# Division of attention's sums moved to GpSimd, with its other work and the steps of three chains placed anew

## What is computed

```python
xn = (x - mean(x)) / sqrt(var(x) + 1e-5)
q = rope((xn @ Wqa @ Wqb).reshape(b, s, 16, 8))
k, v = split((xn @ Wkva @ Wkvb).reshape(b, s, 4, 8, 2))   # 4 heads of k and v serve 16 of q
w = softmax(where(causal, -inf, q @ k.T * 8 ** -0.5))
attn = (w @ v).reshape(b, s, 128) @ Wout + bout
# fp4 quantization in blocks of 16 of the last dimension, of activations and weights
scale = max(max|block| / 6, 1e-12); q4 = GRID[searchsorted(MID, |block / scale|)] * sign * scale
h = silu(q4(xn) @ q4(w_gate).T) * (q4(xn) @ q4(w_up).T)    # 352 wide
out = x + attn + q4(h) @ q4(w_down).T
```

## Time and profile before

| | us |
|---|---|
| median of 3 runs | 797.62 |
| lowest and highest | 795.21, 798.21 |
| the profiled execution's own time | 797.94 |
| its span, first to last instruction | 795.9 |

### The profile page before, as it was taken

How to read it: one execution, slowest core, us unless ns; L and a number is a source line. 1 busy time by engine, 2 the same in 40 slices (tenths; PEclk the granted TensorE clock), 3 DMA queues, 4 the chain that set the end, 5 groups by cost and what they waited for, 6 DMA issues and landing times.

```text
span 795.9 us, 18365 instructions
## 1 busy us (share of the span) xinstructions
PE 722.8 (91%) x6453; PEld 442.3 (56%) x6453; DVE 644.0 (81%) x1390; ACT 535.1 (67%) x1154; POOL 612.3 (77%) x708
## 2 busy tenths in 40 slices
PE   2467889999999999999999999999999999998986
PEld 1233455665656565665656565565656665665434
DVE  6569788989888888989888988889888988878412
ACT  2213686867777777777776767777776867676672
POOL 5534597878889797878889797878889797856662
PEclk9998899999999999999999999999999999999998
DMA  4423233233334343243334343343434333341111
GB/s 113 115 68 88 73 86 102 86 108 110 96 92 116 104 118 96 89 117 98 103 99 119 88 116 96 91 115 96 108 99 116 87 117 93 93 102 38 56 49 35
DMA packets 85028, 75.48 MB, mean 95 GB/s; under 512 B 28642, under 2 KB 67010, under 8 KB 84938
## 3 DMA queue, kind: packets, MB, share of 16 engines
q1 hardware_dynamic: 84938, 74.32, 34.3%
HBM read 40.45 MB, written 27.25 MB: 85 GB/s over the span
## 4 chain that ended last, share of the span: by engine, by line
PE 39%; POOL 32%; ACT 11%; DVE 7%; issue 6%; DMA 3%; SPq 2%; POOLq 0%; DVEq 0%; ACTq 0%
PE pv_ps L1160 10%; POOL P L554 9%; PE exp_ps L1139 7%; POOL h L564 5%; PE max_ps L1124 5%; ACT P L961 5%; POOL h L567 5%; POOL h L570 4%; PE misc_ps L1184 3%; PE max_ps L1125 3%; PE misc_ps L1192 3%; DVE neg_max L737 3%; PE misc_ps L1209 3%; POOL q_split L645 2%; POOL rstd L596 2%
## 5 line engine op out<-in xcount | busy, mean ns | idle before, releaser
L737 DVE TENSOR_REDUCE neg_max<-max_ps 128x1 f32<-128x512 f32 (+3 forms) x768 | 429.9, 593 | 87.1 <-PE max_ps L1125 85.2
L961 ACT ACTIVATE P<-exp_ps 128x512 f32<-128x512 f32 x512 | 294.9, 599 | 167.7 <-PE exp_ps L1139 166.6
L1139 PE MATMUL exp_ps<-Q,K 128*128 128x512 bf16 (+3 forms) x1024 | 244.0, 301 | 10.3 <-ACT P L961 6.5
L1124 PE MATMUL max_ps<-K,Q 128*128 128x384 bf16 (+2 forms) x768 | 199.2, 278 | 18.9 <-DMA Kd<-K 11.7
L1125 PE MATMUL max_ps<-Kd,Q 128*128 128x128 bf16 x1024 | 191.3, 221 | 2.1 <-DVE neg_max L737 2.0
L554 POOL TENSOR_SCALAR_AFFINE_SELECT P<-P 128x512 f32<-128x512 f32 x256 | 161.8, 667 | 26.8 <-ACT P L964 26.8
L1160 PE MATMUL pv_ps<-P,V 128*32 128x512 f32 (+3 forms) x2048 | 163.9, 438 | 1.9 <-POOL P L554 0.8
L1124 PEld LDWEIGHTS max_ps<-K,Q 128*128 128x128 bf16 x768 | 75.9, 100 | 93.3 <-DVE neg_max L737 47.2
L1125 PEld LDWEIGHTS max_ps<-Kd,Q 128*128 128x128 bf16 x1024 | 98.4, 100 | 46.1 <-issue 22.7
L1139 PEld LDWEIGHTS exp_ps<-Q,K 128*128 128x128 bf16 x1024 | 79.7, 98 | 48.4 <-ACT P L961 27.1
L585 POOL TENSOR_TENSOR h<-gate_sb,up_half 128x352 f32<-128x352 f32 x64 | 59.6, 932 | 58.7 <-DVE gate_sb L750 58.6
(11 more groups left out here) (128 smaller groups left out, 974.1 us busy)
## 6 DMA issues: line engine op xcount, KB each, us to landing
Q<-q_scr SPq DMA_DIRECT2D x64, 224.0 KB
o_scr<-oT SPq DMA_DIRECT2D x31, 256.0 KB, 2.6
q_scr<-q_split SPq DMA_DIRECT2D x16, 384.0 KB, 2.6
Kd<-K SPq DMA_DIRECT2D x64, 96.0 KB
x_in<-x SPq DMA_DIRECT2D x16, 256.0 KB, 4.5
q_scr<-q_split SPq DMA_DIRECT2D x16, 256.0 KB, 2.9
x_res<-x SPq DMA_DIRECT2D x16, 256.0 KB, 5.7
out<-y SPq DMA_DIRECT2D x32, 128.0 KB, 4.3
```

The costliest lines, as they stand in the source:

```text
L737: nc.vector.tensor_reduce(neg_max[:, pr // 4, heads[0]:heads[0] + len(heads), pr % 4, i], max_ps[r % 3][:, 0:len(heads) * n].rearrange("p ...
L961: nc.scalar.activation(P[g % 2][:, hh + r % 2, col:col + 512], ps[:, :], ACT.Exp, scale=SCALE).then_inc(exp_done, 1)
L1124: nc.tensor.matmul(ps[:, col:col + d], Qt, Kt[:, half, g, 0:d], start=True, stop=True)
L1139: last = nc.tensor.matmul(exp_ps[n % 2][:, col:col + width], K[par][:, half, pr // 2, kb * 128:(kb + 1) * 128], Q[par][:, pr, kb * 128:S], ...
```

## The change

- GpSimd no longer makes var_eps, neg_mean, shift, the copies of V and x_bias; of the statistics it keeps the power. VectorE makes var_eps (slot 3) and shift (slot 4's end, one instruction).
- The division `onT` goes from VectorE (slot 5) to GpSimd, ahead of the fourth h product.
- GpSimd's step 0 on h stands ahead of the first h product, not behind x's steps 1 to 3.
- V has three buffers, and VectorE copies v from PSUM straight into it, in two instructions; v_stage goes.
- bout becomes row 96 of the third chunk of the down projection's weights, with a row of ones in hqT, set once on VectorE. x_res is added directly, and SP loads it in the pass that uses it.
- ScalarE's powers of h go from behind tiles (2, 2), (2, 3), (2, 4), (3, 2) to (1, 0), (1, 2), (1, 4), (2, 2), x's from (0, 0) to (0, 2). The pieces of xn go from tiles 0 to 3 to tiles 0, 2, 3, 4 of slot 5.
- On VectorE the second half of h's magnitudes stands behind the maxima of tiles 3 and 4 of slot 4, two of four bn_stats at the end of slot 1, and hidden_max(T, 2) in slot 5.

The diff, without the declarations of tiles and semaphores:

```diff
@@ -64,7 +64,7 @@
-H_POWERS = [(2, 2), (2, 3), (2, 4), (3, 2)]
+H_POWERS = [(1, 0), (1, 2), (1, 4), (2, 2)]
 PV_BLOCKS = ((0, 3), (1, 2))
@@ -347,7 +346,7 @@
             for dst, src in (
-                (bout_sb[:, :], bout.partition_broadcast(128)),
+                (wdT[FC[2][1]:FC[2][1] + 1, 2, :], bout.unsqueeze(0)),
                 (w_raw[:, 768:768 + F], wdown),
@@ -475,11 +474,13 @@
+                    T.prev().misc_wait(sp, misc_read, "out1")
+                    sp.dma_start(x_res[:, :, :], x[T.batch(-1)].rearrange("(c p) e -> p c e", p=128)).then_inc(x_res_loaded, 16)
                     return finish()
-                if T.has(0):
...
-                    T.wait(sp, x_bias_done, 1, 0, 0)
-                    sp.dma_start(x_res[:, :, :], x[T.batch(0)].rearrange("(c p) e -> p c e", p=128)).then_inc(x_res_loaded, 16)
+                if T.has(-1):
...
+                    T.prev().misc_wait(sp, misc_read, "out1")
+                    sp.dma_start(x_res[:, :, :], x[T.batch(-1)].rearrange("(c p) e -> p c e", p=128)).then_inc(x_res_loaded, 16)
                 scatter_sums(T, -1, 1)
@@ -585,17 +586,23 @@
-            def statistics(T):
+            def normalize(T):
...
+                if not T.has(-1) or T.t0 == LAST_T:
+                    return
+                T.wait(pool, o_loaded, 32, -1, 32)
+                T.wait(pool, o_inv_in, 32, -1, 32)
+                if T.has(-2):
...
+                    T.prev().misc_wait(pool, misc_filled, "out1")
+                nc.gpsimd.tensor_tensor(onT[:, :], o_raw[:, :], o_spread[:, :], ALU.mult).then_inc(o_normed, 1)
...
+            def deviation(T):
...
                     return
-                T.wait(pool, mv_done, NT, 3, NT)
-                nc.gpsimd.tensor_scalar(var_eps[:, :], bn_mv[:, :, 1], EPS, None, ALU.add).then_inc(var_done, 1)
-                nc.gpsimd.tensor_scalar(neg_mean[:, :], bn_mv[:, :, 0], -1.0, None, ALU.mult).then_inc(var_done, 1)
-                T.wait(pool, var_done, 2, 3, 2)
+                T.wait(pool, var_done, 1, 3, 1)
                 nc.gpsimd.tensor_tensor(rstd[:, :], var_eps[:, :], half_neg[:, :], ALU.pow).then_inc(rstd_done, 1)
-                T.wait(pool, rstd_done, 2, 3, 1)
-                nc.gpsimd.tensor_tensor(shift[:, :], neg_mean[:, :], rstd[:, :], ALU.mult).then_inc(rstd_done, 1)
@@ -605,6 +612,8 @@
                 split_rest(T, 0, 1)
+                if T.has(0):
+                    quantize(T, 0, 0, *hs)
                 hidden(T, 0)
@@ -613,21 +622,11 @@
                     nc.gpsimd.tensor_tensor(blocks(w_raw[:, :]), blocks(w_raw[:, :]), spread(w_inv[:, :]), ALU.mult).then_inc(w_step, 1)
-                if T.has(0):
-                    quantize(T, 0, 0, *hs)
                 hidden(T, 1)
...
                     causal(T, 0, 0)
-                if T.has(1):
...
-                    T.prev().misc_wait(pool, misc_read, "v")
-                    if T.has(-1):
-                        T.wait(pool, pv_done, KVH, -1, KVH)
-                    for s in range(2):
-                        nc.gpsimd.tensor_copy(V[T.par(1)][:, :, s::2, D * s:D * s + D],
-                                              v_stage[:, :, :].rearrange("p c (g d) -> p c g d", g=KVH)[:, :, s::2, :]).then_inc(v_ready, 1)
                 if T.has(2):
@@ -650,8 +649,9 @@
                     nc.gpsimd.tensor_tensor(k_split[:, 2, :], k_rest[:, :], k_split[:, 1, :], ALU.subtract).then_inc(k_pool, 1)
-                statistics(T)
+                deviation(T)
                 split_rest(T, 1, 0)
+                normalize(T)
                 hidden(T, 3)
@@ -661,11 +661,6 @@
                     quantize(T, 0, 3, *hs)
-                if T.has(0):
-                    T.wait(pool, x_res_loaded, 16, 0, 16)
-                    T.misc_wait(pool, misc_read, "out1")
-                    nc.gpsimd.tensor_tensor(x_bias[:, :, :], x_res[:, :, :],
-                                            bout_sb[:, :].unsqueeze(1).to_broadcast([128, NT, E]), ALU.add).then_inc(x_bias_done, 1)
                 if T.has(3):
@@ -689,14 +684,20 @@
-            def magnitudes(eng_wait, mag, sem_):
...
+            def magnitude_bits(mag, sem_):
                 m = mag.bitcast(U16)
...
                 nc.vector.tensor_scalar(m, m, 0x7F80, 0x0040, ALU.bitwise_and, ALU.bitwise_or).then_inc(sem_, 1)
...
+            def magnitude_floor(eng_wait, mag, sem_):
...
                 eng_wait(sem_, 1)
                 nc.vector.tensor_scalar(mag, mag, 1.5 * 2.0 ** 22, None, ALU.max).then_inc(sem_, 1)
...
+            def magnitudes(eng_wait, mag, sem_):
...
+                magnitude_bits(mag, sem_)
+                magnitude_floor(eng_wait, mag, sem_)
@@ -767,28 +768,17 @@
-            def normalize(T):
...
-                if not T.has(-1):
-                    return
-                T.wait(dve, o_loaded, 32, -1, 32)
-                T.wait(dve, o_inv_in, 32, -1, 32)
-                if T.has(-2):
...
-                    T.prev().misc_wait(dve, misc_filled, "out1")
-                nc.vector.tensor_tensor(onT[:, :], o_raw[:, :], o_spread[:, :], ALU.mult).then_inc(o_normed, 1)
...
             def output(T, n):
...
                 if n == 0:
-                    T.wait(dve, x_bias_done, 1, -1, 1)
+                    T.wait(dve, x_res_loaded, 16, -1, 16)
...
                 nc.vector.tensor_tensor(y[:, c, :], misc_ps[0][:, 0:2 * E].rearrange("p (c e) -> p c e", c=2),
-                                        x_bias[:, c, :], ALU.add).then_inc(misc_read[0], 1)
+                                        x_res[:, c, :], ALU.add).then_inc(misc_read[0], 1)
@@ -855,6 +845,10 @@
                 reduces(1, 5)
+                if T.has(3):
+                    T.wait(dve, x_loaded, 16, 3, 16)
+                    for c in range(2):
+                        nc.vector.bn_stats(bn_raw[:, c, :], x_in[:, c, :]).then_inc(bn_done, 1)
@@ -877,9 +871,7 @@
                     T.wait(dve, x_loaded, 16, 3, 16)
...
-                    T.wait(dve, var_done, 2, 2, 2)
-                    for c in range(NT):
+                    for c in range(2, NT):
                         nc.vector.bn_stats(bn_raw[:, c, :], x_in[:, c, :]).then_inc(bn_done, 1)
@@ -889,27 +881,43 @@
                         nc.vector.bn_aggr(bn_mv[:, c, :], bn_raw[:, c, :]).then_inc(mv_done, 1)
-                reduces(3, 4, 5)
+                reduces(3, 4)
+                if T.has(3):
+                    T.wait(dve, mv_done, NT, 3, NT)
...
+                    T.wait(dve, rstd_done, 2, 2, 1)
+                    nc.vector.tensor_scalar(var_eps[:, :], bn_mv[:, :, 1], EPS, None, ALU.add).then_inc(var_done, 1)
+                reduces(3, 5)
                 if T.has(2):
...
-                    T.wait(dve, v_ready, 2, 1, 2)
-                    nc.vector.tensor_copy(v_stage[:, :, :], misc_ps[1][:, 0:128].rearrange("p (c n) -> p c n", c=NT)).then_inc(misc_read[1], 1)
+                    if T.has(-1):
...
+                        T.wait(dve, pv_done, KVH, -1, KVH)
+                    for odd in range(2):
+                        nc.vector.tensor_copy(V[T.third(2)][:, :, odd::2, D * odd:D * odd + D],
+                                              misc_ps[1][:, 0:128].rearrange("p (c g d) -> p c g d", c=NT, g=KVH)[:, :, odd::2, :]
+                                              ).then_inc(v_ready if odd == 0 else misc_read[1], 1)
...
                     T.wait(dve, h_powers, NT, 0, NT)
-                    magnitudes(lambda s, n: T.wait(dve, s, 2, 0, n), h_mag[:, :], h_mags)
+                    magnitude_bits(h_mag[:, :], h_mags)
                 reduces(4, 1, 2)
                 gated(T, 3)
-                reduces(4, 3)
-                hidden_max(T, 2)
-                reduces(4, 4, 5)
+                reduces(4, 3, 4)
+                if T.has(0):
+                    magnitude_floor(lambda s, n: T.wait(dve, s, 2, 0, n), h_mag[:, :], h_mags)
+                reduces(4, 5)
...
                     store_weights()
+                if T.has(3):
+                    T.wait(dve, rstd_done, 2, 3, 1)
+                    nc.vector.scalar_tensor_tensor(shift[:, :], bn_mv[:, :, 0], -1.0, rstd[:, :],
+                                                   ALU.mult, ALU.mult).then_inc(rstd_done, 1)
                 reduces(5, 0)
-                normalize(T)
+                hidden_max(T, 2)
                 reduces(5, 1, 2)
@@ -935,6 +943,8 @@
+            nc.vector.memset(hqT[FC[2][1]:FC[2][1] + 1, 2, :], 1.0).then_inc(ones_row, 1)
             nc.vector.memset(last_sums[:, :, 0:HALF], 0.0).then_inc(dve_marks, 1)
@@ -1036,8 +1046,8 @@
                     split_high(T, 1, 0)
-                if slot == 5 and r < NT:
-                    normalize_x(T, r)
+                if slot == 5 and r != 1:
+                    normalize_x(T, max(r - 1, 0))
                 if (slot, r) == (3, 1) and T.has(2):
@@ -1054,7 +1064,7 @@
                     nc.scalar.activation(q_split[:, 1, :], q_rest[:, :], ACT.Copy).then_inc(q_casts, 1)
```

(9 more changed lines are left out.)

25 lines of the change are left out of this document (12 added, 13 removed).

## The result

| | before | after |
|---|---|---|
| median, us (4 runs each) | 796.41 | 804.01 |
| lowest and highest | 795.02, 798.21 | 803.03, 804.33 |
| the profiled execution and its span | 797.94, 795.9 | 804.25, 802.0 |
| PE / DVE / ACT / POOL busy | 722.8 / 644.0 / 535.1 / 612.3 | 726.0 / 650.1 / 534.9 / 589.4 |

The change makes the kernel slower: the ratio is 1.0095, with a 95% interval of 1.0074 to 1.0116. The forecast was 797.0, no change that can be measured; the time lies inside the range, on the side of rival B.

The account below looks back on a forecast made before the run. Waits, not any engine's sum, bound the kernel: a loop through TensorE, ScalarE and GpSimd closing at h. Twelve periods gave about -0.5 us, ramp and tail -0.1, so 797.3, stated as 797.0 against the median; range 787 to 808.

Parts of the forecast that it names:

- rival B: VectorE-GpSimd locks line up in slots 4 and 5, TensorE loses time: +0.85 us per period, 807 us; chance 0.28.
- Ramp and tail: First and last iterations: start +0.4 us, TensorE's wait for h at t0 = 0 -1.2, plus the last iterations; together -0.1.
- Step 1: ScalarE, slot 0: x's powers behind the third exponent tile let th0 and up0 come earlier; -0.3 us per period.
- Step 2: GpSimd's first h step ahead of the first h product holds x's magnitudes on VectorE; +0.65 us per period.
- Step 4: Statistics: GpSimd keeps only the power, VectorE gets var_eps and shift; -0.82 us per period.
- step 5: Division moved to GpSimd: +1.25 us per period there, -0.41 from the h step no longer beside it on VectorE.
- step 3: ScalarE's powers of h in slots 1 and 2: -0.39 us; x_scale without its wait: up to 0.1 in slot 7.
- TensorE still waits for h: Sign named for the forecast being right: in the changed kernel TensorE would still be waiting for h.
- Step 6: VectorE's second operation on h's magnitudes, moved later: costs nothing if it meets the short power, rival B if the division.
- B's first wait: VectorE's var_eps coming after q_split has started waits 1.1 us and slot 4 slides; a coin's toss within 0.1 us.
- Tail: Last iterations: -1.1 us each at t0 = 13 and 14, +2.8 at 15, where h's powers delay the sums' copy.
- Rival C: Relief does nothing because TensorE is full (98% busy): 797 to 799 us; chance 0.45 together with the forecast.

Follow-up runs that it names:

- e3: Changed kernel with all four bn_stats back in VectorE's slot 3 in every pass; 796.63 us, ratio 0.9987 to the kernel before.
- e2: Kernel before, with only two of the four bn_stats moved to the end of VectorE's slot 1, in every pass; 803.95 us, ratio 1.0081.
- e1: Changed kernel with all four bn_stats back in VectorE's slot 3 in the second pass alone; 796.96 us, ratio 0.9994 to the kernel before.
- e4: Changed kernel with the load of sequence 1's input issued ahead of the masks' constants; 796.57 us, ratio 0.9999 to the kernel before.
- c3: The s2 kernel with ScalarE's powers of x behind the first tile of slot 0 again; 788.07 us, ratio 0.9886 to the kernel before.
- s2: The e1 kernel with GpSimd's scaling of h behind x's three steps again and ScalarE's powers of h in slots 2 and 3; 783.69 us, ratio 0.9842.
- s6: The e1 kernel with the second operation on h's magnitudes (the floor) directly behind their bits again; 787.19 us, ratio 0.9890 to the kernel before.
- p_pe_extra: The e1 kernel with TensorE's four transposes of the quantized x issued twice in slot 5; 797.20 us, ratio 1.0012 to the kernel before.
- c1: The s2 kernel with the floor of h's magnitudes directly behind their bits as well; 788.20 us, ratio 0.9899 to the kernel before.

## Why the prediction was wrong, point by point

**The failed step is one that is not in the prediction.** "The change, by steps" counts seven edits and leaves out one that "The change" lists: two bn_stats of VectorE moved from slot 3 to the end of slot 1. "Ramp and tail" gives the start +0.4, for a memset and the statistics, and nothing for this move. Its own method asks of each moved step what it waits for and what is queued behind it; here that is the load of the next sequence's input, and q_sin, the first link of the chain that brings q to TensorE. In the steady period the load is an iteration ahead, and the edit is free (e3, e2). In the second pass it lands at 28.44, q_sin comes 6.9 late, and the time goes up by 6.6 to 7.4 (e2; the kernel after against e1 and e4). With this one edit out of the way the changed kernel takes 796.96 us, and the forecast was 797.0.

That agreement is luck in part, as the terms show:

- *The stretch of the earlier trace rows*: "one steady period" of 43.60 us is 0.75 short of one. Over a whole period TensorE is busy 43.47 of 44.35, still 98%, so nothing hung on it.
- *Step 1, -0.3 per period*: measured -0.34 (c3), and slot 0 is 0.36 shorter than before.
- *Step 2, +0.65*: the mechanism came as written; the second x_mag operation takes 0.91, where 1.0 to 1.1 was said, and slot 1 is 0.59 longer than before the change and than in s2.
- *Step 4, -0.82, and step 5, +1.25 - 0.41, on GpSimd*: the division takes 1.27 there, as taken. With step 3 (-0.39 - 0.1) these terms come to -0.47, and slot 7, where TensorE had waited for h, is 0.57 shorter. What it did not have is slot 5, 0.43 longer, where the floor meets the division: the loop has gone elsewhere. GpSimd's scaling of x waits 2.5 us for VectorE each period, and TensorE has no wait for h left. That was a named sign ("TensorE still waits for h"), and it was wrong: GpSimd's savings were larger than needed, and by the trace the loop closed over VectorE in slots 1 and 5. No run takes back the V copies, x_bias, the bias row or the statistics, so their single shares are not shown.
- *Step 6, "nothing, if it meets the short power; rival B, if it meets the division"*: it meets the division. It starts 0.2 after the power has ended, 0.01 behind the division. s6 prices this at 0.58 per period, the chance period of e4 at 0.52. B was right about this link, about the shift behind it (0.55) and about ScalarE's xn held by that (0.68), and wrong about the cause and the sum. B's first wait, var_eps behind q_split, came in one of twelve periods (1.03 at 244.46) and left that one at 44.44, as the floor still ended 0.38 behind the division; in the others var_eps takes 0.16, as at 377.55, between the GpSimd product that ends at 377.44 and the one that starts at 377.61. In e3_all_late it came in all twelve (0.91 to 1.08), and the period was 44.45 to 44.49 all the same, save two. So this wait does not set the period while the floor is held behind the division anyway. B had it a toss within 0.1 us, and the trace bears that out.
- *The sum of the period, -0.05 to 0*: measured +0.08 against the plain period of before (44.43 against 44.35), or nothing over twelve, as before has one period longer by 1.15. Without the floor's meeting alone it is 43.87 (s6), or -0.48. So my terms together gave 0.4 to 0.5 too little gain, and that hid a meeting of 0.58 that I had left to rival B. In s2, where neither x's magnitudes nor the floor is held, the period is 0.81 below that of before.
- *Tail*: t0 = 13, 14 and 15 were to be -1.1, -1.1 and +2.8. Measured -1.41, -0.55 and +1.35. At t0 = 15 TensorE waits 1.20 for h at 783.80. From GpSimd's division (771.73) to there it is 12.07, and 12.0 was said. But the division comes 23.0 behind the first transposes of h of t0 = 14, where I had 768.2, or 24.5 behind them: ScalarE's copy of the sums, oT, starts 12.57 behind those transposes where it was 12.31 before, so the powers delayed it by 0.26 and not by 1.17, and that the round trip behind it is shorter does the rest. The sign and the chain were right.
- *The sum of ramp and tail* was written as -0.1; its terms, -1.2 - 1.1 - 1.1 + 2.8 + 0.4, give -0.2. It changes nothing.
- *Rival C, TensorE full anyway*: in slot 5 it is not, as 0.43 us more of its work changed nothing (p_pe_extra); for the other slots this stays open.
- *Start without the bn_stats*: e1 has the first transposes of h 0.43 earlier than before. Said were +0.4 and -1.2, together -0.8.

The Trainium skill (VectorE: DVE Perf Modes, What auto-detection actually checks) was cited for var_eps, a strided float32 operation of 4 columns. The trace agrees that it can be held: it takes 1.03 at 244.46 in the kernel after and 0.91 in c1, where the unhindered one takes 0.16. In eleven of twelve steady periods of the kernel after it fell into a gap, and it did not decide the case.

## What to carry to other kernels

Ask of every instruction that is moved up an in-order queue what it waits for in each pass and not in the steady one alone: the first passes, where loads still stand behind constants, are the place where a move that is free later costs all of its wait once, and a chain follows behind it. What an instruction costs that shares a lock with another engine is set by what it meets: read who starts first, by tenths of a microsecond, and expect an edit that moves one engine by such an amount to make or break other meetings further down (the reordering on GpSimd and ScalarE of s2 gave a kernel 13 us faster than e1). An engine that carries 69% of the chain of waits and is busy for 98% of a period need not be the one that sets it; a small dose of extra work tells, for the place where it is put. Compare whole periods, from mark to mark: the same clock times in two runs are not the same part of a period.
